# Cross attention in a decoder layer: rows of a quad's half four partitions apart in the split tile, three apart in the stack

## What is computed

```python
def xattn(target, source, target_mask, source_mask, Wq, bq, Wk, bk, Wv, bv):   # SIZE 256, HEADS 16, HEAD_DIM 16
    q = einsum('oc,bct->bot', Wq, target) + bq[None, :, None]
    k = einsum('oc,bcs->bos', Wk, source) + bk[None, :, None]
    v = einsum('oc,bcs->bos', Wv, source) + bv[None, :, None]
    q, k, v = (z.reshape(b, HEADS, HEAD_DIM, 512) for z in (q, k, v))
    dot = einsum('bhdt,bhds->bhts', q, k) / math.sqrt(HEAD_DIM)
    mask = target_mask[:, :, :, None] * source_mask[:, :, None, :]
    dot = mask * dot - (1.0 - mask) * 1e6
    amap = softmax(dot, axis=-1) * mask
    return einsum('bhts,bhds->bhdt', amap, v).reshape(b, 256, 512)
```

## Time and profile before

| | us |
|---|---|
| median of 3 runs | 2863.63 |
| lowest and highest | 2856.78, 2868.21 |
| the profiled execution: span, first to last instruction | 2864.8 |
| TensorE busy in the span | 2602.2 (91%) |
| VectorE, ScalarE, GpSimd busy | 1885.6, 1455.5, 996.1 |
| self attention | about 0 to 1378 |
| cross attention, prologue to last batch | about 1378 to 2360 |
| end of the routing, experts | about 2360 to 2865 |

### The profile page before, as it was taken

One profiled execution on the slowest core, in us unless ns is written; L12 is line 12 of the kernel. 1 busy time (PEld: TensorE's weight loads), 2 busy tenths in 40 slices (PEclk: granted clock), 3 DMA queues, 4 the chain that ended last, 5 costly groups with the idle time before them and its releaser, 6 DMA issues. The chain is left out here.

```text
span 2864.8 us, 50062 instructions
## 1 busy us (share of the span) xinstructions
PE 2602.2 (91%) x14768; PEld 1801.6 (63%) x14769; DVE 1885.6 (66%) x3845; ACT 1455.5 (51%) x2868; POOL 996.1 (35%) x1178
## 2 busy tenths in 40 slices
PE   7999999999999999999489999898999876399997
PEld 6888888888788888888333333333333322277776
DVE  6556655555655444555488888888888877576765
ACT  4334433334433333344157767776777665355554
POOL 1112221111211111122426556555665546433332
PEclk9999999999999999999689999999999998699998
DMA  3201222202211011110657777777777777755554
GB/s 147 74 15 58 73 73 73 73 31 102 89 59 54 35 59 44 44 59 30 123 92 127 136 138 139 125 134 141 139 129 133 139 153 254 260 102 104 110 107 85
DMA packets 141571, 290.70 MB, mean 101 GB/s; under 512 B 39600, under 2 KB 42544, under 8 KB 135872
## 3 DMA queue, kind: packets, MB, share of 16 engines
q1 hardware_dynamic: 113184, 223.38, 33.3%
q0 software_dynamic: 23664, 58.09, 9.6%
q10 hardware_dynamic: 4656, 8.40, 1.0%
HBM read 147.82 MB, written 81.68 MB: 80 GB/s over the span
## 5 line engine op out<-in xcount | busy, mean ns | idle before, releaser
L1577 DVE TENSOR_REDUCE b_negmax<-b_ps_s 128x2 f32<-128x1024 f32 x512 | 615.5, 1220 | 105.8 <-PE b_ps_s L1762 100.2
L1376 ACT ACTIVATE b_probs<-b_ps_s 128x1024 f32<-128x1024 f32 x512 | 517.2, 1020 | 229.0 <-PE b_ps_s L1773 226.4
L278 POOL TENSOR_SCALAR probs<-probs,rinv 128x256 f32<-128x256 f32 x256 | 242.0, 945 | 1094.1 <-DVE rinv L435 1094.1
L312 ACT ACTIVATE probs<-ps_s,negmax 128x128 f32<-128x128 f32 x256 | 94.1, 368 | 485.0 <-DVE negmax L428 485.0
L1762 PE MATMUL b_ps_s<-b_stack 54*128 54x512 f32 x1024 | 231.4, 449 | 92.0 <-ACT b_probs L1376 42.9
L1773 PEld LDWEIGHTS b_ps_s<-b_stack 56*128 56x128 f32 x1024 | 97.2, 186 | 309.2 <-issue 195.7
L1784 PE MATMUL b_ps_o<-b_probs,b_v_stack 128*32 128x512 f32 x2048 | 281.5, 622 | 1.5 <-ACT b_probs L1376 1.1
L1773 PE MATMUL b_ps_s<-b_stack 56*128 56x512 f32 x1024 | 254.9, 494 | 27.8 <-ACT b_probs L1376 14.4
L543 PE MATMUL ps_proj<-xT_h,wq_h 128*128 128x512 f32 x512 | 215.7, 421 | 0.0
L2467 POOL DMA_INDIRECT out<-e_y,e_place_int x71 | 118.8, 1674 | 250.9 <-DMA out<-e_y,e_place_int 210.6
L543 PE MATMUL ps_proj<-xT_h,wq_l 128*128 128x512 f32 x512 | 201.7, 394 | 0.0
(11 more groups left out here) (334 smaller groups left out, 6628.6 us busy)
## 6 DMA issues: line engine op xcount, KB each, us to landing
b_stack<-b_split SPq DMA_DIRECT2D x240, 128.0 KB
e_row<-rows_by_expert SPq DMA_DIRECT2D x71, 258.0 KB, 2.9
b_out_tiles<-row_sum_inverses SPq DMA_DIRECT2D x64, 256.0 KB
x<-acc SPq DMA_DIRECT2D x15, 1024.0 KB, 5.0
b_stack<-b_late SPq DMA_DIRECT2D x96, 128.0 KB
x_in<-in_x SPq DMA_DIRECT2D x8, 1024.0 KB, 8.3
normalised_x_split<-xT_h SPq DMA_DIRECT2D x8, 1024.0 KB, 10.0
normalised_x_split<-xT_l SPq DMA_DIRECT2D x8, 1024.0 KB, 11.1
```

What stands on the lines that cost most here:

```text
L278: nc.gpsimd.tensor_scalar(probs[:, s, P:3 * P], probs[:, s, P:3 * P], rinv[:, s, 1:2], None, ALU.mult).then_inc(probs_done, 1)
L312: nc.scalar.activation(probs[:, s, 0:P], ps_s[s][:, 0:P], ACT.Exp, bias=negmax[:, s, 0:1], accum_out=rowsum[:, s, 0:1])
L1376: nc.scalar.activation(probs[:, k % 2, p, :, :], ps[:], ACT.Exp, scale=0.25).then_inc(e_done, 1)
L1577: nc.vector.tensor_reduce(negmax[:, k, p, :], ps[:], AX.X, ALU.max, negate=True).then_inc(m_reduced, 1)
```

## The change

The 32 rows of a quad no longer stand in one block. A row of quad q, half i goes to partition 64i + 4d + q of `split`, d from 0 to 15 (`spread`): a half's rows stand four partitions apart over 64 partitions. In the stack its three groups are interleaved: row d of group n goes to partition 64i + n + 3d, three apart over 48 partitions. `late` becomes a tile of 128 partitions, of which every fourth is used. The columns of the split weights and the biases are permuted to match. Bytes, number of DMAs, their order and the order of all instructions stay the same on every engine; the eight ScalarE and eight VectorE instructions that split the weights write their 128 columns with a step of four in place of one after another.

```diff
--- before.py
+++ after.py
@@ -762,7 +762,7 @@
         cs = [sb(f"c_{s}", [P, CT, T], F32R) for s in "hl"]
         raw = {n: sb(f"raw_{n}", [P, 2, T]) for n in "qk"}
         tile = sb("split", [P, 4, 2, T], F32R)
-        late = sb("late", [2 * DH, 4, 2, T], F32R)
+        late = sb("late", [P, 4, 2, T], F32R)
         mask_b = sb("mask_b", [P, T])
         mask_col = sb("mask_col", [P, TBL])
         mask_r = sb("mask_r", [P, TC])
@@ -955,15 +955,17 @@
 
             return t.rearrange("c (q d p i) -> c p q i d", q=QUADS, d=DH, p=2, i=2)[:, p]
 
+        def spread(q, i):
+
+            return slice(SIDE * i + q, SIDE * (i + 1), QUADS)
+
         def stack_half(b, q, i, eng):
 
-            base = 2 * DH * q if q < QUADS - 1 else 0
             of = tile if q < QUADS - 1 else late
-            src = slice(base + DH * i, base + DH * (i + 1))
             for n, (query, key) in enumerate(PAIRS):
-                r = SIDE * i + DH * n
-                eng.dma_start(stack[r:r + DH, q, :, :, :].bitcast(F32),
-                              of[src, query:key + 1:key - query].bitcast(F32)).then_inc(
+                r = SIDE * i + n
+                eng.dma_start(stack[r:r + AUX:len(PAIRS), q, :, :, :].bitcast(F32),
+                              of[spread(q, i), query:key + 1:key - query].bitcast(F32)).then_inc(
                                   half_stacked if (q, i) == (0, 1) else stacked[q], 16)
 
         def load_bias(eng, n, src):
@@ -972,8 +974,7 @@
                 heads = src.rearrange("(u d p i) h -> h u i d p", u=2, d=DH, p=2, i=2)
                 for q in range(QUADS):
                     for i in range(2):
-                        r = 2 * DH * q + DH * i
-                        eng.dma_start(bias[n][r:r + DH, :], heads[q // 2, q % 2, i]).then_inc(bias_loaded[n], 16)
+                        eng.dma_start(bias[n][spread(q, i), :], heads[q // 2, q % 2, i]).then_inc(bias_loaded[n], 16)
 
         W_AT = {"k": 0, "q": 1, "v": 2}
         W_PARTS = {"k": 1, "q": 2, "v": 3}
@@ -1029,7 +1030,7 @@
 
                     if not (static(b) and b == 0):
                         wait_alone(sp, stacked[QUADS - 1], STACKS[QUADS - 1] * b, (consts, 4))
-                    sp.dma_start(late[:].bitcast(F32), tile[P - 2 * DH:P].bitcast(F32)).then_inc(late_copied, 16)
+                    sp.dma_start(late[QUADS - 1:P:QUADS].bitcast(F32), tile[QUADS - 1:P:QUADS].bitcast(F32)).then_inc(late_copied, 16)
 
                 def stack_negmax(b, q):
                     wait_alone(sp, nm_rows_done, QUADS * b + q + 1, (consts, 4))
@@ -1326,7 +1327,7 @@
                     for k in range(CT):
                         for p in range(2):
                             ins = nc.scalar.activation(
-                                w[name][0][:, k, p * P:(p + 1) * P].rearrange("c (q i d) -> c q i d", q=QUADS, i=2),
+                                w[name][0][:, k, p * P:(p + 1) * P].rearrange("c (i d q) -> c q i d", q=QUADS, i=2),
                                 head_cols(w_stage[:, W_AT[name], k, :], p), ACT.Copy)
                     ins.then_inc(w_high, 1)
 
@@ -1504,9 +1505,9 @@
                         for p in range(2):
                             cols = (slice(None), k, slice(p * P, (p + 1) * P))
                             ins = nc.vector.tensor_tensor(
-                                w[name][1][cols].rearrange("c (q i d) -> c q i d", q=QUADS, i=2),
+                                w[name][1][cols].rearrange("c (i d q) -> c q i d", q=QUADS, i=2),
                                 head_cols(w_stage[:, W_AT[name], k, :], p),
-                                w[name][0][cols].rearrange("c (q i d) -> c q i d", q=QUADS, i=2).bitcast(F32), ALU.subtract)
+                                w[name][0][cols].rearrange("c (i d q) -> c q i d", q=QUADS, i=2).bitcast(F32), ALU.subtract)
                     ins.then_inc(w_low, 1)
 
                 def normalise(b):
```

## The result

| | before | after |
|---|---|---|
| median, us | 2863.96 | 2847.73 |
| lowest and highest, 5 runs each | 2856.78, 2869.90 | 2842.14, 2850.50 |
| ratio of the times, 95% interval | | 0.9922 [0.9898, 0.9947] |
| profiled span | 2864.8 | 2840.4 |
| TensorE, VectorE busy in the span | 2602.2, 1885.6 | 2598.5, 1876.4 |

The two profiled executions are 24.4 us apart. That is more, because the profiled execution of the changed kernel is the fastest of its five (2842.14 us), so what follows accounts for 24.4 us and not for 16.2.

The account below looks back on a forecast made before the run. Cross attention was taken as mostly bound by TensorE, ScalarE close behind, with a DMA last once in most batches. Terms −3.2 − 4.9 − 16.2 − 4.6 + 0.5 = −28.4 us gave 2835 us for the median, range 2816 to 2866.

Parts of the forecast that it names:

- term 3: The 13 batches after the first: 56.35 us each in place of 57.60 on average, 16.2 us saved (0 to 27).
- Term 1: Prologue: TensorE's 21.60 us wait for the stack shortens as its 1565 KB move at 272 GB/s, 3.2 us saved (0 to 4.4).
- 2, first batch: First batch of cross attention: 56.35 us in place of 61.20, 4.9 us saved.
- Term 4: Last two batches: half of TensorE's 9.2 us of DMA waits beside the routing's loads goes, 4.6 us saved (0 to 12).
- Term 5: Weight split: its eight ScalarE and eight VectorE instructions write with a step of four, 0.5 us added (0 to 3).
- model batch: Batch from 1934.13 to 1990.48 before the change, 56.35 us, taken as a batch's cost when the stack comes in time.
- A: Rival, stack moves: no change, since the engines set the slow pace or neighbouring DMAs already spread the load; 2864 us, chance 0.20.
- B: Rival, batches: the stack comes in time, but waits for VectorE's maxima take its place; 2850 us, chance 0.20.
- C: Rival, turn (2, 0) and reciprocals: spread moves hold up other traffic, half 0 lands after over 8.3 us; 2879 us, chance 0.07.

Follow-up runs that it names:

- the copy moved: Against the changed kernel, the 512 KB copy to `late` issued later, behind half 0 of quad 1 instead of half 0 of quad 0: 2826.99 us.
- the two slow layouts: The same later copy to `late` in the kernel before (blocks), 2883.52 us, and in the kernel with only the source side spread, 2939.90 us.
- the step of two: Against the changed kernel, a half's source rows two apart inside the quad's own 32 partitions, `late` copied from partitions 96 to 127: 2871.39 us.
- the probe with one queue: Changed kernel plus prologue bursts of half 1, half 0 and the `late` copy from SP's queue, five layouts; half 0 after 7.09 us in the change, 9.13 in blocks.

## Why the prediction was right, and where it was not

**The time.** I forecast 2835 us and a range of 2816 to 2866; it is 2847.73, 1.6 us under the 2849.3 from which I would have called it no change.

**The mechanism** that I named is a part of it. The stack moves land earlier and the waits at (2, 0) go or shrink: where TensorE waited there, it was mostly until 8.3 to 8.5 us after the first issue of half 0 before, and until 7.5 to 7.7 after. These 0.8 us are less than the 1.4 to 2.8 that I had worked out, though the factor of 1.5 for the busy time came out. Another part is VectorE: in 1500 to 2200 TensorE's waits for the stack fell by 6.0 us and those for the maxima by 7.2, and with the stack side alone only the latter fell. I had named this way in term 3 (the small DMA of the row sums, "so it too should come earlier"), but gave it no price of its own. And the clock fell behind the wait at that turn in three of the 13 batches where it had fallen in seven.

By terms, from the two profiles:

| term | forecast | measured |
|---|---|---|
| pace of the stack moves | 1.5 | 1.52 by busy time per MB; a half alone 5.96 to 4.40 us, 1.35 |
| 1, prologue | −3.2 | −0.2 |
| 2, first batch | −4.9 | −6.2 |
| 3, 13 batches | −16.2 | −21.8 |
| 4, last two batches | −4.6 | −5.6, then +5.7 in the rest of the routing |
| 5, weight split | +0.5 | +0.2 |

The terms leave out the stretch between the first use of the stack and the first batch's mark. There TensorE has the same waits, but from 20 to 30 us behind the first use its granted clock is 0.69 where it was 0.89 before: it came back to its upper level later. With that, and with the prologue's −0.2, it is 1.4 us longer from the start of cross attention to the first batch's mark. Start to last mark is then +1.4 − 6.2 − 21.8 = −26.6, as in the table above. That the sum of −28.4 came near the 24.4 us of the profiles is in part luck: terms 2, 3 and 4 gained 8 us more than forecast, and terms 1 and 5, this stretch, the start and the end together 12 less.

**Term 1 failed.** I took the bytes from 1416 to the first use and divided them by a higher pace. After, the wait is 21.1 us where I had said 18, and the three stretches of pure stacking moved this (fourth stretch: 1424 to 1430):

```profile
1416.00:1420.00 4.00, 0.00 (x0) 0.00 (x0) 0.00 (x0) 0.00 (x0) 3.97 (x10) 0.50 0.97 192
1420.00:1424.00 4.00, 0.00 (x0) 0.00 (x0) 1.53 (x4) 1.06 (x1) 2.59 (x8) 0.50 1.02 161
1424.00:1430.00 6.00, 2.44 (x8) 1.18 (x8) 2.34 (x3) 2.57 (x3) 5.59 (x5) 0.50 1.04 225
```

192, 161 and 225 GB/s against 164, 186 and 177, and nowhere the 272 that I took. With the second load issued behind the stack, the first use came 5.9 us earlier: what stood ahead in the queue counts for more in this wait than the pace of the moves did here.

**Terms 2 and 3 were too small.** The model batch of 56.35 us was not the floor. Its clock was 1.00 throughout, but 0.85 us of waits for the stack were in it; after the change most batches take 55.0 to 55.6, and with the copy moved 54.9 was reached in most. The bound that I gave, 2.1 us a batch, held for the changed kernel (1.7), and the kernel with the copy moved went past it (2.6). Twelve short waits remained, and three of the 13 batches paid for them with the clock.

**Term 4 came and went.** The last two batches gained 5.6 us, near the forecast. My step "TensorE paces what follows, so the gain reaches the end whole" failed: from the last maxima matmul to the end it takes 520.6 us before and 526.3 after. In the table of the cuts this part has two lengths: 519.7 to 522.2 in seven kernels, 526.3 to 528.8 in four, with one profiled execution of each. The four longer ones have TensorE's row of waits at the routing's matmul for `c_xT` at 15.4 to 20.4 us (the changed kernel's 15.4 stands above). The kernel with only the copy moved has:

```profile
PE b_ps_p L2289 <- ACT c_xT L2132: 4.6, 5, 1.2
```

So TensorE waits some 11 to 16 us more for ScalarE's copies in the routing, and the end is some 6 to 8 us longer. What decides between the two wasn't tested.

**Term 5** was nearly nothing: ScalarE's instructions of the weight split take 412 and 418 ns (410 and 412 before), VectorE's 384 and 400 (377 and 376), 0.2 us for all sixteen.

**The check on a rule.** The estimate that I drew from the Trainium skill, page "SBUF — State Buffer", section "Door 1: The DMA port swizzle", was a factor of 1.5, from the source side, with the stack side unchanged. For the change as a whole the busy time agrees (1.52). By its sides it doesn't: alone in the kernel, the source side made it 2% slower, and the stack side, to which I gave no part, brought half of the gain in the batches and most of it by the medians. My reading of the table was off there too: I counted the rows of the three DMAs together, and by the same table the 16 rows of one of them go from four ports, four rows each, to eight ports with at most three. Alone and without other traffic a half gains 0.7 us by the source, 0.2 by the stack and 1.56 by both.

**The rivals.** A (no change) is out: the share fell and the waits went. B (VectorE takes the wait's place) did not happen here: over the whole run the maxima end 8.8 us of waits where it was 16.7 (the 9.1 in the rows are those on L1762 alone; 7.6 more stand on L1773). It is just what happened when the copy was moved in the two slow layouts, through the row sums as B had it. VectorE's waits on the row sums did not shrink in sum: 10.0 us in 7 waits became 10.0 in 12, but each is shorter (at most 2.3, from 3.7), and in the same stretch TensorE waits 1.4 us for the maxima where it was 8.6. C (other traffic held up) did not happen either, but the source side alone did what C describes: half 0 was awaited some 10.0 us after its issue, above C's 8.3, and the batches took 60.69 us. So the 7% that I gave C was for something that does happen, with the source alone and less so with the step of two (8.8 to 9.1 us); the changed kernel stayed clear of it.

## What to carry to other kernels

A layout of on-chip rows for DMA is to be judged by when the awaited transfers land in the full kernel; neither the DMA share nor the move alone gave the order here: the source side cut the share from 0.75 to 0.64 and lost 2%, the stack side left it and gained. Look at every wait that ends at such a transfer, and not only at the one that the change was made for: here the waits for VectorE's maxima shrank by as much as those for the stack. Try both sides together, and then look again at the order of the queue: one 512 KB copy moved further behind an awaited half took another 20.7 us off the median (8.0 of them seen in the batches), yet added as much in the layout before. Where the clock falls behind a short wait, the batch is about 1.2 us longer than with as short a wait at full clock; but it fell behind only three such waits of eleven.

## What the runs showed of the hardware that was not expected

- A half (three DMAs, 384 KB, within on-chip memory) takes 5.96 us from 16 adjacent partitions to 16, 5.24 with only the source four apart, 5.76 with only the destination three apart, 4.40 with both, and 4.50 with a source step of two. The two sides together gain 1.56, more than their sum of 0.92.
- Behind six stack moves in blocks, SP took 1.24 us to issue the copy to `late`, and 0.60 in the layout of the change; the six took 5.07 and 3.83 us to issue, in the probe with one queue. The issuing went with the source's rows and not with how slow the moves were: 3.80 us with the source alone, whose half 0 came after 8.52 us, and 5.01 with the stack alone (9.24).
- The same pattern of moves that was as fast as the change in three probes (the step of two: 4.50 against 4.40, 7.19 against 7.09, 6.31 against 6.31 us) had the kernel 24 us slower (2871.39 against 2847.73).
